# The last 3x3 convolution of a four-block residual network, cut into three parts instead of two

## What is computed

```python
x = x + _L0_conv_ref(_gn(x), ...)
x = x + _L1_conv_ref(_gn(x), ...)
x = x + _L2_conv_ref(_gn(x), ...)
x = x + _L3_conv_ref(_gn(x), ...)
return x
```

```python
w1_eff = jnp.einsum('e,eoihw->oihw', alpha, w1)
w2_eff = jnp.einsum('e,eoihw->oihw', alpha, w2)
out = _conv3x3(x, w1_eff)
out = jax.nn.relu(_bn(out, bn1_gamma, bn1_beta, bn1_mean, bn1_var))
out = _conv3x3(out, w2_eff)
out = _bn(out, bn2_gamma, bn2_beta, bn2_mean, bn2_var)
return jax.nn.relu(out + x)
```

## Time and profile before

| | |
|---|---|
| median of 3 runs | 419.45 us |
| profiled execution | 420.92 us |
| its span in the profile | 419.1 us |
| TensorE matmul busy | 386.3 us (92%) |
| VectorE busy | 273.9 us (65%) |
| last convolution, first to last matmul | 391.8 to 410.7 us |
| last OT of VectorE ends | 416.6 us |

### The profile page before, as it was taken

How to read it: one execution, slowest core, us unless ns; L and a number is a source line. 1 busy time by engine, 2 the same in 40 slices (tenths; PEclk the granted TensorE clock), 3 DMA queues, 4 the chain that set the end, 5 groups by cost and what they waited for, 6 DMA issues and landing times.

```text
span 419.1 us, 8316 instructions
## 1 busy us (share of the span) xinstructions
PE 386.3 (92%) x3210; PEld 266.4 (64%) x3210; DVE 273.9 (65%) x479; ACT 57.1 (14%) x97; POOL 96.6 (23%) x230
## 2 busy tenths in 40 slices
PE   0799799999999999999999999979899989799991
PEld 0344588888888888888888888732237662267670
DVE  4981367777877887787787788864343276831155
ACT  0721000000000000000000000041004107752200
POOL 6687500588820000000000000015001006700000
PEclk9999799999999999999999999999999999999998
DMA  6276768155545535626714400049920000000023
GB/s 206 65 179 153 177 146 215 27 138 121 139 113 126 160 86 136 176 61 146 182 34 104 127 2 0 1 101 204 235 51 2 4 2 0 2 2 5 3 85 119
DMA packets 19650, 40.17 MB, mean 96 GB/s; under 512 B 7329, under 2 KB 8225, under 8 KB 19041
## 3 DMA queue, kind: packets, MB, share of 16 engines
q1 hardware_dynamic: 18848, 38.63, 36.5%
q10 hardware_dynamic: 768, 1.08, 1.0%
HBM read 4.62 MB, written 2.10 MB: 16 GB/s over the span
## 4 chain that ended last, share of the span: by engine, by line
PE 72%; SPq 9%; DVE 9%; DMA 5%; issue 2%; ACT 1%; POOL 0%; DVEq 0%; POOLq 0%
PE ps L771 21%; PE ps L772 21%; PE ps L773 7%; SPq L334 5%; PE ps L962 5%; PE ps L946 4%; PE ps L806 3%; PE ps L823 3%; PE ps L891 2%; PE ps L915 2%; DMA LS<-HS 2%; SPq L386 2%; DMA X<-in_x 2%; SPq L371 2%; DVE RED L1022 1%
## 5 line engine op out<-in xcount | busy, mean ns | idle before, releaser
L771 PE MATMUL ps<-WA,HS 128*128 128x512 f32 x396 | 160.6, 406 | 1.4 <-DMA LS<-HS 1.4
L772 PE MATMUL ps<-WB,LS 128*128 128x512 f32 x396 | 157.7, 398 | 0.0
L1040 DVE TENSOR_TENSOR PROD<-ps,PT 128x512 f32<-128x512 f32 x132 | 91.2, 691 | 46.3 <-PE ps L773 42.0
L1022 DVE TENSOR_REDUCE RED<-PROD 128x32 f32<-128x512 f32 x132 | 89.2, 676 | 0.0
L771 PEld LDWEIGHTS ps<-WA,HS 128*128 128x128 f32 x396 | 75.8, 191 | 20.5 <-issue 1.5
L772 PEld LDWEIGHTS ps<-WB,LS 128*128 128x128 f32 x396 | 75.7, 191 | 16.5
L773 PE MATMUL ps<-WC,TS 96*128 96x512 f32 x132 | 52.9, 401 | 0.0
L456 POOL MEMSET IMG<- 128x67 f32 x1 | 0.2, 154 | 153.9 <-DVE X L1029 153.9
L658 ACT ACTIVATE P<-ps 128x256 f32 x15 | 5.8, 384 | 207.5 <-PE ps L786 207.5
L806 PE MATMUL ps<-REPL,ONE 128*128 128x256 f32 x120 | 29.2, 397 | 1.8 <-DVE X L1224 1.3
L823 PE MATMUL ps<-SK,WE 128*32 128x512 f32 x256 | 28.2, 594 | 1.9 <-DMA SK<-IMG 1.9
(11 more groups left out here) (199 smaller groups left out, 325.3 us busy)
## 6 DMA issues: line engine op xcount, KB each, us to landing
HS<-HI SPq DMA_DIRECT2D x72, 96.5 KB, 2.1
LS<-HS SPq DMA_DIRECT2D x6, 1158.0 KB, 6.8
TS<-LO SPq DMA_DIRECT2D x72, 80.0 KB, 2.1
SK<-IMG SPq DMA_DIRECT2D x32, 131.8 KB, 2.8
HS<-LO SPq DMA_DIRECT2D x24, 96.5 KB, 2.1
LS<-LO SPq DMA_DIRECT2D x24, 96.5 KB, 2.1
X<-in_x SPq DMA_DIRECT2D x4, 512.0 KB, 5.6
out_x<-OT SPq DMA_DIRECT2D x8, 256.0 KB, 2.0
```

Of the source, the lines that this page charges most:

```text
L771: pe.matmul(ps[b][:, :], px(HS, dy * PW), WA[:, dy, :], start=(dy == 0), stop=False)
L772: pe.matmul(ps[b][:, :], px(LS, dy * PW), WB[:, dy, :], start=False, stop=False)
L1022: ve.tensor_reduce(RED[j % 2][:, 32 * b:32 * b + 32], PROD[b % 2][:, :].rearrange("p (o e) -> p o e", e=E0), AX.X, ALU.add).then_inc(sum_d ...
L1040: ve.tensor_tensor(PROD[b % 2][:, :].rearrange("p (o e) -> p o e", e=E0), ps[b][:, :].rearrange("p (o e) -> p o e", e=E0), para.rearrange( ...
```

## The change

The two halves of 8 rows become three parts of 8, 4 and 4 rows of each quarter. PARTS gives first row, rows and first bank of each: rows 4 to 11 into banks 0 to 3, rows 12 to 15 into banks 4 to 7, rows 0 to 3 into banks 0 to 3 again. Part 1 needs no halo row, so the wait for the halo copies stands before parts 2 and 3. Part 3 uses the banks of part 1, so for each quarter it waits for affine4_done, which T raises. Each part has its own conv4_done, its own four T and OT, and its own four output transfers, of 128 x 512 or 128 x 256 elements.

```diff
+PARTS = ((4, 8, 0), (12, 4, 4), (0, 4, 0))
+N_OUT = 4 * len(PARTS)
...
-            for n in range(NCH):
-                k = 2 * (n % 4) + 1 - n // 4
+            for n in range(N_OUT):
+                r0, nr, _ = PARTS[n // 4]
+                a = (r0 + QR * (n % 4)) * W
                 sp.wait_ge(out_rows_done, n + 1)
-                sp.dma_start(out[:, k * CH:(k + 1) * CH], OT[n % 4][:, :]).then_inc(out_written[n % 4], 16)
+                sp.dma_start(out[:, a:a + nr * W], OT[n % 4][:, 0:nr * W]).then_inc(out_written[n % 4], 16)
...
-            for n in range(2):
-                h = 1 - n
-                pe.wait_ge(halo_by_vector, 3 * n + 3)
-                pe.wait_ge(halo_by_scalar, 3 * n + 3)
+            for n, (r0, nr, bank) in enumerate(PARTS):
+                if n:
+                    pe.wait_ge(halo_by_vector, 6)
+                    pe.wait_ge(halo_by_scalar, 6)
                 for t in range(TAPS):
                     for q in range(4):
+                        if n == 2 and t == 0:
+                            pe.wait_ge(affine4_done, q + 1)
                         p = slice(32 * q, 32 * q + 32)
                         for b in range(B):
-                            ins = pe.matmul(ps[4 * n + q][32 * b:32 * b + 32, :], W3[p, 1, t, :], rows(HQ[p, b, :], CR * h + t % 3, CR, t // 3),
+                            ins = pe.matmul(ps[bank + q][32 * b:32 * b + 32, 0:nr * W], W3[p, 1, t, :], rows(HQ[p, b, :], r0 + t % 3, nr, t // 3),
                                             start=(t == 0), stop=(t == TAPS - 1))
                 ins.then_inc(conv4_done, 1)
...
-            for n in range(NCH):
-                k = 2 * (n % 4) + 1 - n // 4
+            for n in range(N_OUT):
+                r0, nr, bank = PARTS[n // 4]
+                r, m = r0 + QR * (n % 4), nr * W
                 ve.wait_ge(conv4_done, n // 4 + 1)
-                ve.scalar_tensor_tensor(T2[n % 4][:, :].rearrange("p (r c) -> p r c", c=W), ps[n][:, :].rearrange("p (r c) -> p r c", c=W),
-                                        S3[:, 2:3], rows(IMG, 1 + k * CR, CR), ALU.mult, ALU.add).then_inc(affine4_done, 1)
+                ve.scalar_tensor_tensor(T2[n % 4][:, 0:m].rearrange("p (r c) -> p r c", c=W), ps[bank + n % 4][:, 0:m].rearrange("p (r c) -> p r c", c=W),
+                                        S3[:, 2:3], rows(IMG, 1 + r, nr), ALU.mult, ALU.add).then_inc(affine4_done, 1)
                 ve.wait_ge(affine4_done, n + 1)
                 if n >= 4:
                     ve.wait_ge(out_written[n % 4], 16 * (n // 4))
-                ve.scalar_tensor_tensor(OT[n % 4][:, :], T2[n % 4][:, :], S3[:, 4:5], X[:, k * CH:(k + 1) * CH], ALU.max, ALU.add).then_inc(out_rows_done, 1)
+                ve.scalar_tensor_tensor(OT[n % 4][:, 0:m], T2[n % 4][:, 0:m], S3[:, 4:5], X[:, r * W:r * W + m], ALU.max, ALU.add).then_inc(out_rows_done, 1)
```

More of the change, by code:

```diff
@@ L433, in _ @@
                 sp.dma_start(W2B[p, :, :].rearrange("p (x d) o -> p x (d o)", x=3), w2b[:, g, :, :].rearrange("(x c) d o -> c x (d o)", x=3)).then_inc(w_l2, 16)
-            for n in range(NCH):
-                k = 2 * (n % 4) + 1 - n // 4
+            for n in range(N_OUT):
+                r0, nr, _ = PARTS[n // 4]
+                a = (r0 + QR * (n % 4)) * W
                 sp.wait_ge(out_rows_done, n + 1)
-                sp.dma_start(out[:, k * CH:(k + 1) * CH], OT[n % 4][:, :]).then_inc(out_written[n % 4], 16)
+                sp.dma_start(out[:, a:a + nr * W], OT[n % 4][:, 0:nr * W]).then_inc(out_written[n % 4], 16)
             for i in range(4):
-                sp.wait_ge(out_written[i], 16 * NCH // 4)
+                sp.wait_ge(out_written[i], 16 * N_OUT // 4)
         @block.gpsimd
```

## The result

The change made the kernel slower. The kernel before and the changed one were run 19 times each, the ratio of their times is 1.0083, 95% interval 1.0043 to 1.0123: **+3.5 us** (1.8 to 5.2), 425.83 us in the median against 424.20 in these runs. Set on the 419.45 us of the forecast this is 422.9; I had said 419.1, and at most 422.0. The ratio leaves out executions more than 1.5% above the fastest of their kernel, so it is not the ratio of the two medians, and the profiled execution of the changed kernel is one of those left out. Both kernels spread over some 8 us (419.2 to 427.4 before, 423.3 to 431.6 after), so the cause has to be read from the stage and not from whole times.

What follows compares the result with a forecast made beforehand. The end was set by TensorE's last handover, VectorE's remaining work and 2 us of transfer. TensorE +1.8 us and VectorE 2.15 less gave -0.35 us, from 419.45 to 419.1 us, range 417.6 to 422.0.

Steps and rivals of the forecast that it cites:

- The first part: Last convolution's part 1: same size as the old first half, costs nothing, VectorE again starts T at 401.72.
- VectorE's part: T and OT behind TensorE: 0.27 us saved an instruction, last part 3.75 us instead of 5.89, 2.15 us less.
- The transfers: Output transfers: twelve instead of eight, the queue keeps up, the half-size last one gains 0 to 0.1 us, taken as 0.
- TensorE's part: Matmuls of the narrow parts: 0.60 us a round, 5.4 us a part, TensorE hands over its last part 1.8 us later.
- the picture of the round: TensorE holds about 16 matmuls; two passes plus a fixed 0.14 to 0.19 us give 0.57 to 0.62 us at 256 columns.
- near balance of the other terms: End of the kernel: TensorE's +1.8 us and VectorE's 2.15 less nearly cancel, together -0.35 us.
- rival 1: TensorE's instruction pace, 65 ns a matmul whatever the columns: end 6.9 us later, 426.3 us; chance 0.13.
- Rivals 2 and 3: TensorE's matmuls: bursts longer than a pass, 421.8 us, chance 0.15; columns alone, 417.9 us, chance 0.12.
- The third part's bank wait: Part 3's matmuls wait for T of part 1 on the same banks: free, with 0.3 us to spare.
- What I said would show it: Profile after: T's ninth start near 412.5 after about 1.3 us of waiting, L967 matmuls busy 20.6 us rather than 18.9.
- rival 2: Last convolution's matmuls: start bursts outlast a narrow pass, 0.75 us a round, 421.8 us, matmuls busy 23.4 us; chance 0.15.

Runs made afterwards that it cites:

- run 19: Not a run label: the kernel before and the changed one were run 19 times each; ratio 1.0083, 95% interval 1.0043 to 1.0123.
- e2_cols128: Changed kernel with two of the four rows of parts 2 and 3 left out, 128 columns a matmul; T's first to ninth start 15.22 us.
- e1_loop: Changed kernel with taps 2 and 3 looped three times in parts 2 and 3, in place of taps 2 to 7; T's first to ninth start 11.28 us.
- e11_six_taps: Changed kernel with taps 5 to 7 left out of parts 2 and 3, written out; 9.7 us to TensorE's last matmul.
- e6_cols384: Changed kernel with six rows instead of four in parts 2 and 3, 384 columns a matmul; T's first to ninth start 16.11 us.
- e9_cols448: Kernel before with one of eight rows left out of its second half, 448 columns a matmul; T's first to fifth start 8.05 us.
- e8_pool: Kernel before with T reordered ahead of OT, conv4_done raised per quarter, and one second-half OT moved to GpSimd; ratio 0.9968 (0.9926 to 1.0010).

## Why the prediction was wrong, point by point

- **The first part**: right. 9.90 us to T's first start in both.
- **VectorE's part**: right. 0.48 us an instruction (0.27 saved), 3.75 us at the end as said, 2.14 less than before.
- **The transfers**: nearly. The last transfer, of half the size, lands in 1.71 us instead of 2.01, and the end behind the last OT is 0.24 us shorter; I had taken 0 and at most 0.1. I had also read that every issue of before but the first lands after 2.0 us: of the first four, beside the matmuls, three took longer (3.2, 2.4 and 3.3 us). Nothing hung on that; in the changed kernel transfers there took up to 3.9 us, and no OT waited for one.
- **TensorE's part**: this is the step that failed. The forecast was 0.60 us a round, 10.8 us for both narrow parts. At 256 columns the picture of the round nearly held: in the loop, where no stop is seen, it is 0.627 us, 11.28 in all, and the 0.5 us too little is the small miss. At 128 columns it did not hold: there 128 records took as long as at 256 (e2_cols128). What was missing from the sum is the supply of instructions, a term that I had put at nothing without looking at it. 288 narrow matmuls are 4.5 pieces of program, of which about one had come in ahead; TensorE could go on with a new one only every 3.9 to 4.0 us, each held 2.3 to 2.8 us of work, and the rest, 3.3 us of standstill and some 0.5 for starting again, is 15.13 - 11.28 = 3.85 us. Without it the change would have been at 11.28 - 9.01 - 2.14 - 0.24 = -0.1 us, no difference, and e1_loop shows that: from the last convolution's first matmul to the span's end it has 27.19 us, where before has 27.30. So the forecast's near balance of the other terms was right, and the sign was lost on the term left out.
- **The rivals**: rival 1 was the nearest, and I had left it out of the range. Its sign and its point of decision were good ("from 39 ns a matmul on": the changed kernel took 15.13 / 288 = 53), its mechanism was not, and so its price, 6.9 us, was too high: it took the wide part's pace, 65 ns, where 3.9 us for 64 matmuls is 61, and knew of no piece loaded ahead. The 62 ns that the Trainium skill, "TensorE: Matmul & The Clock Gate", section "Wait — 56ns, not 53.3ns?", states for each MATMUL without hardware decode give, as an estimate, 64 x 62 = 4.0 us for a piece, which looks like the spacing of the pieces. But e1_loop ran the same number of matmuls of the same width at 39 ns each, so what held here is no cost of a matmul. My argument against rival 1, that 16 records started within 0.28 us, was sound for a cost per matmul and said nothing of how fast new instructions arrive: 16 matmuls are a quarter of a piece. The page of before has the pieces (q8, 23 of them, 0.38 MB), which I did not use. That row gives their size and not how fast they can follow one another, so it would have raised the question of the rival and not have answered it. Rivals 2 and 3 did not happen.
- **The third part's bank wait**: 0.3 us to spare was right in kind; with less work in part 2 it becomes real (e11_six_taps).
- **What I said would show it**: for rival 2 I had put 23.4 us of busy matmuls, and the profile has 25.0 us from first to last matmul (398.15 to 423.16), of which 21.7 busy. The standstill within the matmuls was not on my list.

## What to carry to other kernels

Before cutting matmuls into narrower ones, count instructions as well as columns: this written-out float32 code needed some 3.9 us for each 256 TensorE instructions, 64 matmuls here, once more than about two such pieces followed one another, and 64 matmuls of 512 columns in 16 tiles were just above it at 4.2. Idle time of TensorE with "issue" as its releaser and the same number of records between the gaps is the mark of it; here a loop took it away. To shorten a tail behind the last matmul, first look at the order of what follows it: one piece ahead and a signal per quarter gave 1.1 us in the stage without a single matmul more.

## What the runs showed of the hardware that I had not expected

- Program pieces: 256 instructions each; after a stop TensorE goes on every 3.66 to 4.28 us in straight code, whatever the columns (changed kernel 3.91 and 4.00, e2_cols128 3.66 and 4.28, e6_cols384 3.87 and 3.73), and 1.3 to 1.5 us after a piece has come in. 2.25 pieces of 3.6 us ran without a stop (e9_cols448).
- A loop was the faster form. The Trainium skill, "Runtime: NRT & Kernel Launch", section "Instruction fetch mechanics", warns that a taken branch to a target outside the two pages at hand has to wait for that page, and names this as one reason why kernels prefer full unrolling. The loop's body here, 32 matmuls or half a piece, is shorter than a page. It ran three times in each of two parts at 39 ns a matmul without a gap, and the unrolled form at 53 with gaps.
- With 128 columns, 128 records still took 2.8 us, 44 ns a matmul, as with 256 columns between stops, though the loop runs at 39 with 256. What sets this pace within a piece was not tried and stays open.
- GpSimd and VectorE at the same time (e8_pool): one VectorE instruction with two inputs in SBUF took 1.75 us instead of 0.74 and ended 0.55 us after GpSimd's addition, which took 1.83. VectorE's T, with one input in PSUM, kept its 0.74 to 0.75 us beside GpSimd's maximum.
